# Summing the scan's state products: GpSimd adds two pairs into one block, TensorE sums one block per two steps

## What is computed

```python
def step(hst, xs):
    d_t, B_t, C_t, u_t = xs
    dA = jnp.exp(d_t[:, :, None] * A)
    hst = hst * dA + (d_t * u_t)[:, :, None] * B_t[:, None, :]
    y_t = jnp.einsum('bdn,bn->bd', hst, C_t)
    return (hst, y_t)
...
y = ys.transpose(1, 0, 2) + xc * Dp
y = y * jax.nn.silu(z)
```

## Time and profile before

| | |
|---|---|
| median of 3 runs | 5972.65 us (5970.45 to 5973.8) |
| the profiled execution's own time | 5973.68 us |
| its span, first to last instruction | 5971.9 us |
| mean granted TensorE clock | 0.940 of full |
| busy share of the span | PE 88%, DVE 85%, ACT 62%, POOL 66%, weight loads 50% |
| DMA | 1216.99 MB, mean 204 GB/s |

### The profile page before, as it was taken

One profiled execution on the slowest core, in us unless ns is written; L12 is line 12 of the kernel. 1 busy time (PEld: TensorE's weight loads), 2 busy tenths in 40 slices (PEclk: granted clock), 3 DMA queues, 4 the chain that ended last, 5 costly groups with the idle time before them and its releaser, 6 DMA issues.

```text
span 5971.9 us, 63803 instructions
## 1 busy us (share of the span) xinstructions
PE 5277.8 (88%) x18611; PEld 2975.7 (50%) x18611; DVE 5084.5 (85%) x5978; ACT 3698.7 (62%) x6077; POOL 3913.3 (66%) x2702
## 2 busy tenths in 40 slices
PE   6689999999999999999999999999999999999971
PEld 6245555545555555555555455555545555554541
DVE  5799888988988898988889888888888989888843
ACT  2566666666666666666666666666666666666643
POOL 0677766667766776767677776666766767767620
PEclk9799999999999999999999999999999999999996
DMA  3565555555555555555555555555555555555527
GB/s 125 204 229 206 206 206 198 207 207 205 207 207 205 204 210 205 211 201 212 205 196 211 213 205 201 205 207 196 211 212 204 208 205 207 202 205 212 199 106 285
DMA packets 199104, 1216.99 MB, mean 204 GB/s; under 512 B 27880, under 2 KB 28656, under 8 KB 67696
## 3 DMA queue, kind: packets, MB, share of 16 engines
q1 hardware_dynamic: 194416, 1196.26, 54.4%
q10 hardware_dynamic: 4352, 16.78, 0.7%
HBM read 1158.43 MB, written 54.53 MB: 203 GB/s over the span
## 4 chain that ended last, share of the span: by engine, by line
PE 38%; DVE 27%; ACT 19%; issue 13%; DMA 1%; POOL 1%; DVEq 1%; SPq 0%; ACTq 0%; POOLq 0%
PE psE L812 13%; PE psA L812 11%; DVE hs L486 11%; DVE psD L482 10%; PE psT L812 6%; ACT da L678 5%; ACT p L724 4%; PE psT L984 4%; DVE nm L511 3%; ACT pt L688 3%; PE psY L812 2%; ACT L647 1%; ACT L749 1%; ACT sz L650 1%; PE psD L812 1%
## 5 line engine op out<-in xcount | busy, mean ns | idle before, releaser
L301 POOL TENSOR_TENSOR pa<-hs,rows_all 128x1024 f32<-128x1024 f32 x1024 | 2410.4, 2354 | 1580.5 <-DVE hs L486 1577.8
L482 DVE TENSOR_TENSOR psD<-rows_all,psU 128x512 f32<-128x512 f32 x2048 | 1416.3, 692 | 70.2 <-POOL hlast L305 1.2
L678 ACT ACTIVATE da<-delta,neg_a 128x512 f32<-128x512 f32 x2048 | 1367.7, 717 | 119.4 <-DVE hs L486 108.7
L486 DVE TENSOR_TENSOR_SCAN hs<-da,hlast,psD 128x512 f32<-128x512 f32 x1024 | 1310.9, 1280 | 36.3
L486 DVE TENSOR_TENSOR_SCAN hs<-da,psD 128x512 f32<-128x512 f32 x1024 | 1248.9, 1220 | 36.1 <-ACT da L678 0.9
L812 PE MATMUL psY<-pa,ident 128*128 128x512 f32 x2304 | 1184.8, 610 | 50.7 <-POOL pa L308 30.5
L308 POOL TENSOR_TENSOR pa<-pa 128x512 f32<-128x512 f32 x896 | 1137.5, 1270 | 35.1
L724 ACT ACTIVATE p<-psE,nm 128x1024 f32<-128x1024 f32 x512 | 569.6, 1112 | 710.2 <-DVE nm L511 710.2
L812 PE MATMUL psA<-pt,va 128*128 128x256 f32 x4096 | 976.0, 387 | 2.6 <-DVE x L529 1.6
L812 PEld LDWEIGHTS psA<-pt,va 128*128 128x128 f32 x4096 | 794.8, 196 | 250.4 <-issue 153.9
L688 ACT ACTIVATE pt<-psT 128x512 f32<-128x512 f32 x1024 | 560.6, 597 | 451.6 <-PE psT L984 445.2
(11 more groups left out here) (180 smaller groups left out, 4564.7 us busy)
## 6 DMA issues: line engine op xcount, KB each, us to landing
rows_all<-bc_scratch SPq DMA_DIRECT2D x1024, 1024.0 KB, 4.7
xin<-x SPq DMA_DIRECT2D x40, 512.0 KB, 5.7
xres<-x SPq DMA_DIRECT2D x64, 256.0 KB, 4.2
x_scratch<-x SPq DMA_DIRECT2D x32, 512.0 KB, 2.9
f_scratch<-fa SPq DMA_DIRECT2D x32, 512.0 KB, 3.2
xres<-x SPq DMA_DIRECT2D x8, 512.0 KB, 3.2
x1g<-x SPq DMA_DIRECT2D x8, 512.0 KB, 3.3
fa<-x SPq DMA_DIRECT2D x8, 512.0 KB, 3.2
```

The source lines that it names most:

```text
L301: pool.tensor_tensor(pa[:, k % PROD, :, :], hs[:, sl, :, :], rows_all[:, slot, 2:4, :], ALU.mult).then_inc(S["prod"], 1)
L482: dve.tensor_tensor(psD[:, :], rows_all[:, slot, j, :], psU[:, :], ALU.mult).then_inc(S["dbu_ok"], 1)
L486: dve.tensor_tensor_scan(hs[:, sl, j, :], da[:, sl, j, :], psD[:, :], hlast[:, h, n_:n_ + 1] if ch else 0.0, ALU.mult, ALU.add).then_inc(S ...
L678: act.activation(da[:, k % 2, j, :], delta[:, h, cols(ch)], ACT.Exp, scale=neg_a[:, h, 2 * q + j:2 * q + j + 1]).then_inc(S["da_ok"], 1)
```

## The change

GpSimd now adds the two halves of `pa` in every slot, also in 14 and 15. In every odd slot it then adds the sum of the even slot before to it. TensorE sums one 512-column block per two steps: `add` does nothing for an even step. The semaphores `added` and `pair_mm` are replaced by `pair`, `quad` and `quad_mm`; the product of step k, which reuses the buffer of step k-4, now waits until the quad that held that buffer is summed, and for even k that is one slot later than before.

```diff
-ADDED = [r for r in range(16) if r not in (14, 15)]
...
                     wait(pool, "h_ok", b, 2 * k + 2)
-                    wait(pool, "pair_mm", b, k - PROD + 1)
+                    wait(pool, "quad_mm", b, k // 2 - 1)
...
-                    if k % NS in ADDED:
-                        wait(pool, "prod", b, k + 1)
-                        pool.tensor_tensor(pa[:, k % PROD, 0, :], pa[:, k % PROD, 0, :], pa[:, k % PROD, 1, :], ALU.add
-                                           ).then_inc(S["added"], 1)
+                    wait(pool, "prod", b, k + 1)
+                    pool.tensor_tensor(pa[:, k % PROD, 0, :], pa[:, k % PROD, 0, :], pa[:, k % PROD, 1, :], ALU.add
+                                       ).then_inc(S["pair"], 1)
+                    if k % 2:
+                        wait(pool, "pair", b, k + 1)
+                        pool.tensor_tensor(pa[:, k % PROD, 0, :], pa[:, (k - 1) % PROD, 0, :], pa[:, k % PROD, 0, :], ALU.add
+                                           ).then_inc(S["quad"], 1)
...
                 def sum_states(b, k):
 
                     group, q = divmod(k, PAIRS)
-                    if q == 0:
+                    if q == 1:
                         wait(pe, "g_ok", b, group)
-                    parts = 2
-                    if k % NS in ADDED:
-                        wait(pe, "added", b, len(ADDED) * (k // NS) + ADDED.index(k % NS) + 1)
-                        parts = 1
-                    else:
-                        wait(pe, "prod", b, k + 1)
-                    for j in range(parts):
-                        last = mm(psY[:, :], ident[:, :], pa[:, k % PROD, j, :], start=(q == 0 and j == 0),
-                                  stop=(q == PAIRS - 1 and j == parts - 1))
-                    last.then_inc(S["pair_mm"], 1)
+                    if k % 2 == 0:
+                        return
+                    wait(pe, "quad", b, (k + 1) // 2)
+                    mm(psY[:, :], ident[:, :], pa[:, k % PROD, 0, :], start=(q == 1), stop=(q == PAIRS - 1)
+                       ).then_inc(S["quad_mm"], 1)
```

More of the change, by code:

```diff
@@ L181, in build @@
             u_ok=2 * NCH, dbu_ok=2 * STEPS, da_ok=2 * STEPS, h_ok=2 * STEPS,
-            hlast_ok=STEPS // 2, prod=STEPS, added=NCH * len(ADDED), pair_mm=STEPS, g_ok=2 * NCH,
+            hlast_ok=STEPS // 2, prod=STEPS, pair=STEPS, quad=STEPS // 2, quad_mm=STEPS // 2, g_ok=2 * NCH,
             x1_mm=NCH, x1_ok=NCH, x1g_ok=NCH,
@@ L490, in gate @@
                 def gate(b, ch, h):
-                    wait(dve, "pair_mm", b, NS * ch + PAIRS * (h + 1))
+                    wait(dve, "quad_mm", b, (NS * ch + PAIRS * (h + 1)) // 2)
                     dve.tensor_tensor(g[:, h, cols(ch)], psY[:, :], sz[:, h, cols(ch)], ALU.mult
@@ L638, in front @@
                         h = AT_X.index(r)
-                        wait(act, "pair_mm", fb - 1, NS * (fc + 1))
+                        wait(act, "quad_mm", fb - 1, NS // 2 * (fc + 1))
                         wait(act, "xi_mm", fb, 2 * fc + h + 1)
```

## The result

The changed kernel takes 6078.16 us (median of 4 runs, 6077.73 to 6078.84) against 5971.55 us before (4 runs): 1.0178 of it, 95% interval 1.0161 to 1.0196, so 107 us **slower**. The profiled execution's span is 6076.4 us, 104.5 more than before, and its mean granted TensorE clock fell from 0.940 to 0.907.

The account below looks back on a forecast made before the run. No busy share decides: the chain goes by turns through TensorE, VectorE and ScalarE. On 5973.7 us, -49 + 0 + 0 + 22 + 95 + 59 + 35 = +162 gave 6136 us; range 5980 to 6240 us.

Parts of the forecast that it names:

- (a): TensorE's sum ahead of the `energy` of slot 13 is on the path; dropping it saves 0.79 us x 62 blocks, -49 us.
- (b): GpSimd's extra adds, 12.7 us a block, fit in its waits for the scan; tight at slots 13 to 1: 0 us.
- (c): GpSimd's product for even k waits for a sum one slot back, about 2 us later in slot 4: 0 us.
- (d) slot 1: Gap ahead of `energy` grows from 0.83 to 3.4 us, bringing half clock: 0.8 x 1.91 x 62 = +95 us.
- The price of 1.91 us: Cost of one half-clock stretch at slot 8, taken as 86.82 - 84.91 us between blocks; also used for slot 1.
- (d) slots 1 and 2: Gaps of about 1.1 and 1.5 us bring half clock to `inner0`, the weighings and `residual`; taken at half: +59 us.
- (d) slot 8: In first blocks the gap grows from 3.50 to some 4.3 us, bringing more half-clock stretches: +22 us.
- (d) slot 10: Without the sum between `rows` and `steps`, half-clock stretches come in some 80% of blocks, a little longer: +35 us.

Follow-up runs that it names:

- e7: The kernel before with one quad per block (steps 10 and 11), `steps` over 128 rows and zero matmuls in the gap of slot 7: 5794.3 us.
- e5: The kernel before with the matmul `steps` of slot 10 over 128 rows instead of 8, the added rows zero: 5890.0 us.
- e1: The changed kernel with every matmul taken off TensorE put back at its old place as a matmul by zeros: 5980.4 us.
- e10: The kernel before with 434 more GpSimd adds, in images 1 to 31, into a half of `pa` nobody reads: 5974.3 us, ratio 1.0000.
- e8: The changed kernel with zero matmuls in every old place but that of step 10, 128-row `steps` and the gap of slot 7 filled: 5805.1 us.
- e6: The kernel before with 3 (first block of an image) or 5 (second) zero matmuls in TensorE's idle gap at the end of slot 7: 5865.0 us.
- e2: The kernel before with half of TensorE's sums left out and no GpSimd adds more; output not the reference's: 6073.8 us.
- e3: The changed kernel with two zero matmuls at the place of the two sums of slot 0 alone: 5992.8 us.
- e4: The kernel before with one quad per block: GpSimd adds step 10 to step 11, TensorE drops the sum in slot 12: 5964.5 us.
- e11: The changed kernel with zero matmuls at the old places of slots 0, 1 and 2 (two, one, one): 5980.6 us.

## Why the prediction was right, and where its sum was off

The forecast was 6136 us, slower, by extra half-clock stretches; it is 6078 us, by those. Two of its sizes came out only because errors cancelled; they are named below.

- **(a) The sum ahead of slot 13, -49 us.** Right as a mechanism and in size: 0.71 us a block in e7 against e5, 44 us over 62 blocks. In the changed kernel it can't be seen, being given back in the same piece of the block.
- **(b) GpSimd, 0 us.** Right for the full blocks (e1, e10, and e8 against e7). Wrong for image 0, which the prediction did not look at: 10.5 us. The product of 2.35 us, the add of 1.27 and half a quad add are 4.3 us a step there, where VectorE, with no attention to do, needs less.
- **(c) The new wait, 0 us.** Right: e1 has it, and its full blocks are as long as before. The sum of slot 7 does wait for its quad, in the idle gap, in second blocks.
- **(d) slot 1, +95 us.** Right as a mechanism, 98 us by the means; the size is in part luck. The gap became 2.5 us and not 3.4, since the `centre` ahead of it now waits 0.60 us for ScalarE. The clock fell behind it in 55 of 56 blocks and not in 0.8 of them, though behind the longer gap of 3.50 us it had held in 9 first blocks of 30; so the length of the gap alone does not decide, and the counts at slot 8 were no measure for slot 1. And a stretch costs 1.6 us and not 1.91. 0.8 x 1.91 = 1.53 came near 1.58 because the two errors cancel.
- **The price of 1.91 us.** It was read from unlike blocks. 86.82 us is a second block, 84.91 us a first one, and the two differ without any half clock. `xn` in e7, where these blocks have none:

```profile
2941.75 1.38 DVE L475 TENSOR_TENSOR xn<-xcen,rstd 128x512 f32<-128x512 f32 x1
...
3026.25 1.45 DVE L475 TENSOR_TENSOR xn<-xcen,rstd 128x512 f32<-128x512 f32 x1
...
3110.11 1.39 DVE L475 TENSOR_TENSOR xn<-xcen,rstd 128x512 f32<-128x512 f32 x1
```

  The second block lasts 84.50 us and the first 83.86. So 0.64 of the 1.91 us is no clock at all, and 1.27 us are left for the stretch at slot 8, which agrees with the 1.32 us of e6.
- **(d) slots 1 and 2, +59 us.** This is the step that failed. It was added to the one at slot 1 as if the two were independent. They exclude each other: e2 has one of them in each block and never both, e3 has the second where the first is filled, and in the changed kernel the first comes in 55 blocks and the second in 1. The term is 0. It is as large as the 58 us by which the forecast was too high, because the other misses nearly cancel: (a) +5, image 0 +10.5, slot 1 +3, slot 10 +6, slot 8 -20.
- **(d) slot 8, +22 us.** Off: the half-clock time there did grow, from 5.55 to 6.83 us a block, and all 56 blocks have it, but the piece up to `steps` grew by 0.04 us, 2 us in all. First blocks lost 0.38 us and second blocks won 0.30. The price of 1.91 us was too high, and it was taken to be the same whatever work the stretch falls on. Two of the sums that went (slots 8 and 10) lay in this piece; whether that is why the second blocks won was not tried.
- **(d) slot 10, +35 us.** The stretch came in all 56 blocks instead of 30. With (a) the piece changed by -0.05 us, so it cost what (a) was worth: 0.71 - 0.05 = 0.66 us a block, 41 us. The reason given, the missing sum between `rows` and `steps`, is not shown: e4 has the stretch in 55 blocks with that sum in place, e11 in 56 and e3 in 48 without it. No run takes out that sum alone.

By these, 98 + 2 - 3 + 10.5 is 107.5 us, against 106.6 measured. The first three are means of 56 blocks scaled to 62.

## What to carry to other kernels

Ask of work taken off TensorE what the hole does to its clock: a gap of 2.5 us on a path that TensorE sets cost more than ten matmuls of 0.86 us a block gave. Where TensorE has idle time that can't be used, matmuls by zeros in it, and padding of a small matmul to all rows, are worth trying before any saving of its work; here they made 104 and 80 us alone, and 175 us (3%) together with one saved sum. Price a saved piece with the clock held, since otherwise a stretch elsewhere can give it back, as in e4. And price a slow stretch on blocks that do the same work: here two blocks that differ by 0.64 us of other work made it look half as dear again.

## What was not expected of the hardware

- An edit behind `steps` that is worth 0.7 us moved the number of blocks in which the clock falls at slot 10, which it leaves as it was, from 30 to 55 of 56 (e4), and a filled gap 20 us earlier moved it from 30 to 7 (e6). Why is not shown.
- Behind a matmul of 8 rows, 2 us long, the clock fell in 30 of 56 blocks with 0.14 us of idle time ahead of it; with the rows padded to 128 by zeros it fell in none (e5). Matmuls by zeros held the clock where they filled a gap (e1, e6).
- `xn`, VectorE's instruction with two SBUF operands, waits for GpSimd. With GpSimd idle it takes 0.69 us, and otherwise it ends 0.55 us behind the end of the GpSimd instruction that runs when it starts: so in 63 of 63 cases before and in 59 of 63 after. In the other four GpSimd's add had begun at most 0.04 us earlier or began behind it; there `xn` took 0.67 us and the add 1.65 to 1.82 instead of 1.27. That gives every other length from 0.91 to 2.18 us, by how much of GpSimd's instruction is left. `xn` before, in the set-up, and then GpSimd's product (ending at 271.95 us) and `xn` after, in image 0:

```profile
162.52 0.69 DVE L466 TENSOR_TENSOR xn<-xcen,rstd 128x512 f32<-128x512 f32 x1 [8.38 <-ACT rstd L635]
...
269.61 2.34 POOL L300 TENSOR_TENSOR pa<-hs,rows_all 128x1024 f32<-128x1024 f32 x1
270.32 2.18 DVE L468 TENSOR_TENSOR xn<-xcen,rstd 128x512 f32<-128x512 f32 x1
```

  The Trainium skill, "GPSIMD Engine Reference", section "Specifications", has this clash for such instructions, and the trace agrees.
